# A two-stage graph network on one core: one-pass batch statistics, a normalisation folded into weights, merged matrix products, and a last stage spread over three engines

## The chip, the core and the metric

The kernel runs on 1 core of a Trainium2 chip. The metric is the device time of one launch in microseconds (us). Below, PE is TensorE, DVE is VectorE, ACT is ScalarE, POOL is GpSimd and SP is SyncE, which here only starts transfers. All numbers are fp32.

## What is computed

12,500 nodes with 64 values each, 400,000 edges sorted by `dst` with 32 values each. Three passes over the edges, with weights between them:

```python
# layer 0
msg  = relu(concat([x[dst], x[src], edge_attr, u_per_node[dst]]) @ W1 + b1)
agg  = segment_sum(msg, dst)
x    = layernorm(x + relu(concat([x, agg, u_per_node]) @ W2 + b2))
# layers 1 and 2: h starts as x
def _egnn_conv(h, src, dst, ea, W, b, bias):          # ea = edge_attr @ We + be
    h = h @ W + b
    return relu(segment_sum(h[src] + ea, dst) + h) + bias
def _batchnorm(x, gamma, beta):                       # over all 12,500 nodes
    mu, var = mean(x, axis=0), var(x, axis=0)
    return (x - mu) * rsqrt(var + EPS) * gamma + beta
h = _batchnorm(_egnn_conv(x, ...1), g1, beta1)
h = _batchnorm(_egnn_conv(h, ...2), g2, beta2)
return layernorm(x + h)
```

`u_per_node` is one row for all nodes, since `batch` is all zeros.

## The kernel before, in words

The core runs through a start, and then three times (l = 0, 1, 2) through an edge loop and a node stage. Every engine has its own program; semaphores tie them together, and each engine works its own list in order.

**Start.** DVE and PE find where each block of 128 nodes begins among the edges. POOL gathers rows of `dst` for it (98 gathers, L530) and, when the ranks are known, scatters node rows into the table `ranked` (98, L538). Beside this PE forms, for 14 groups of 7 blocks, three products per block (L602 to L604): node rows by W1's first half, a product of `glob_b` (the row u with a 1 behind it) by `w_glob`, which adds u's share and the bias, and node rows by W1's second half. SP loads `xt`, a group at a time.

**Edge loop** (625 steps of 5 tiles of 128 edges). In each step POOL starts 5 indirect DMAs (L556) that gather source rows of 128 edges each from `source_table`. The ring `message` holds 10 steps. DVE makes the one-hot matrix `hit` (L937), PE multiplies (L666), DVE adds the result into `by_rank` (L952). In layer 0 PE also forms the edge products (L639, L642), with a one-hot `spread` from DVE (L925).

**Node stage** (14 groups of 7 blocks of 128 nodes). PE transposes `by_rank` (L678), ACT copies it out (L762), SP stores it to `sums`. POOL fetches a node's sum by its rank: it copies the ranks of a group from `rank_i` into `node_idx` (L569) and gathers 7 times (L574). DVE builds `cat` from what was fetched (L964, or L968 to L974), PE transposes it (L689), ACT copies the transpose to `cat_t` (L770), PE multiplies by the node weights (L701 to L703 in layer 0, where L703 is again the product of `glob_b`; L705 in layers 1 and 2), DVE applies the relu (L983, L988). In layer 0 a layernorm follows (`after_norm`, L810 to L820, with a square root on ACT, L776) and SP stores the group as the next `source_table`. The groups are pipelined: `fetched` and `cat` have two halves.

**Batch statistics** (layers 1 and 2). PE adds up `conv` over the partitions, a group at a time, with a matrix of ones (L711), one group behind. At the end DVE has the mean (L1015), subtracts it from all 14 groups (L1022), ACT squares each (L789), PE sums the squares (L724), DVE reduces (L1027), ACT takes the root (L794), DVE the reciprocal and the gain (L1029, L1030). In layer 1 DVE then scales and shifts all of `conv` in 7 pairs of groups (L1034, L1035), SP stores each pair as the next `source_table` (L494) and behind the last one loads the first indices (L409). In layer 2, DVE works through 7 pairs: gain, beta, add xn, and a layernorm (L1043 to L1045, then L813 to L820), with a root on ACT (L799); SP writes the pairs out (L500, L502).

The order is written out by hand. The lines that decide the starts named later:

```python
# SP, before the edge loop of layers 1 and 2
if l:
    sp.wait_ge(tile_summed[l - 1], STEPS)
    for n in range(0, CYCLE, TURN):
        load_index(Step(0, n))
    wait_for_table(sp, l)
```

## Time and profile before

| | us |
|---|---|
| time before, median of 3 runs (12688.62 to 12696.25) | 12688.88 |
| the profiled execution, its own time | 12692.79 |
| its span, on which all sums below are made | 12691.0 |
| busy POOL / PE / DVE / ACT | 9386.9 / 6733.1 / 4907.3 / 395.8 |
| first POOL gather of the three edge loops | 300.1, 4448.7, 8545.1 |
| last POOL gather of the three edge loops | 4239.6, 8348.2, 12444.5 |

So some 300 us are the start, three loops of 3900 to 3940 us follow, and after each a node stage: about 209 us, 197 us and 246 us (to the end at 12691.0). Times are microseconds from the span's start unless marked ns. In a timeline row the first number is the start, the second the duration; the bracket is the engine's idle time before it and what ended it. A row "x2" or "x7" covers so many instructions. An fp32 product shows as two matmul records.

### The profile page before, as it was taken

Reading aid. Unit: us, or ns where it says so; the run is one execution under the profiler, and the core shown is the slowest. Engines: PE = TensorE matmul, PEld = TensorE weight load, DVE = VectorE, ACT = ScalarE, POOL = GpSimd, SP = SyncE. Lnnn points to the kernel's source line nnn. Section 1 sums busy time; section 2 is a strip of 40 time slices with the busy share of each in tenths; the row PEclk is TensorE's granted clock in tenths of the full one; section 3 lists DMA queues with packets and bytes.
Section 4 is the critical chain, followed back from the end, with each engine's and each line's share of the span. In section 5 each row is a group of like instructions: output and inputs, shape, how many; then the busy total and the mean of one; then the engine's idle time right before and its main releaser. Section 6 shows DMA issues by size and latency. Waiting matters only on the chain.

```text
span 12691.0 us, 121543 instructions
## 1 busy us (share of the span) xinstructions
PE 6733.1 (53%) x29865; PEld 5780.0 (46%) x29865; DVE 4907.3 (39%) x12980; ACT 395.8 (3%) x790; POOL 9386.9 (74%) x9927
## 2 busy tenths in 40 slices
PE   4888877888878833333333333343333333333334
PEld 4777766677767733333333333333333333333333
DVE  2444444444444333333333333333333333333334
ACT  0000000000000100000000000000000000000000
POOL 6777777777777577777777777767777777777774
PEclk9666667666666555555555555555555555555555
DMA  2444434343444222222222222221111111111111
GB/s 78 100 94 93 95 93 96 92 95 92 98 94 94 65 41 40 41 40 40 40 40 40 41 40 40 40 54 27 27 27 27 27 27 27 27 27 27 27 27 37
DMA packets 1598914, 688.43 MB, mean 54 GB/s; under 512 B 1359841, under 2 KB 1422977, under 8 KB 1598734
## 3 DMA queue, kind: packets, MB, share of 16 engines
q0 software_dynamic: 315680, 328.70, 13.3%
q1 hardware_dynamic: 1283181, 359.10, 12.8%
q8 instruction: 24, 0.39, 0.0%
q14 instruction: 29, 0.24, 0.0%
HBM read 658.74 MB, written 28.14 MB: 54 GB/s over the span
## 4 chain that ended last, share of the span: by engine, by line
POOL 32%; PE 28%; DMA 19%; issue 15%; DVEq 3%; DVE 2%; POOLq 0%; ACT 0%; SPq 0%; ACTq 0%
POOL message L556 30%; PE sum_ps L666 20%; DMA message<-source_table,index 18%; PE pre_ps L642 3%; DVEq L920 3%; PE pre_ps L639 2%; POOL fetched L574 1%; DVE by_rank L952 1%; POOL ranked L538 1%; DVE summed_in L931 0%; PE out_ps L701 0%; PE out_ps L703 0%; PE out_ps L702 0%; PE sum_ps L689 0%; DMA xt<-in_x_t 0%
## 5 line engine op out<-in xcount | busy, mean ns | idle before, releaser
L556 POOL DMA_INDIRECT message<-source_table,index x9375 | 8887.3, 948 | 2947.0 <-issue 2546.7
L666 PE MATMUL sum_ps<-hit,message 128*64 128x128 f32 (+1 forms) x18750 | 4254.6, 408 | 4821.3 <-DMA message<-source_table,index 4746.6
L666 PEld LDWEIGHTS sum_ps<-hit,message 128*64 128x64 f32 (+1 forms) x18750 | 3577.4, 231 | 5348.2 <-DMA message<-source_table,index 4962.0
L952 DVE TENSOR_TENSOR by_rank<-by_rank,sum_ps 64x128 f32 (+1 forms) x9375 | 2628.5, 280 | 4567.1 <-PE sum_ps L666 4277.6
L937 DVE TENSOR_TENSOR hit<-out_ps,edge_place 128x640 f32<-128x640 f32 x1875 | 1526.8, 814 | 1207.2 <-PE sum_ps L666 690.6
L639 PE MATMUL pre_ps<-w_edge,scratch 96*128 96x192 f32 x2500 | 946.9, 473 | 874.6 <-DVE summed_in L931 742.0
L642 PEld LDWEIGHTS pre_ps<-scratch 128*128 128x128 f32 x6250 | 1230.9, 271 | 111.5 <-issue 79.0
L642 PE MATMUL pre_ps<-scratch 128*128 128x64 f32 x6250 | 1278.4, 356 | 0.0
L639 PEld LDWEIGHTS pre_ps<-w_edge,scratch 96*128 96x128 f32 x2500 | 525.5, 262 | 1119.3 <-DVE summed_in L931 790.6
L931 DVE TENSOR_TENSOR summed_in<-pre_ps,message 128x320 f32<-128x320 f32 x625 | 303.1, 485 | 771.7 <-issue 594.1
L925 DVE TENSOR_SCALAR scratch<-edge_cat,lane 128x640 f32<-128x640 bf16 x625 | 344.9, 552 | 603.2 <-issue 593.1
L750 ACT ACTIVATE message<-summed_in 128x320 f32<-128x320 f32 x625 | 293.6, 470 | 3788.2 <-DVE summed_in L931 3756.9
L574 POOL DMA_INDIRECT fetched<-sums,node_idx x294 | 285.4, 971 | 139.9 <-issue 76.8
L762 ACT COPY message<-sum_ps 128x448 f32<-128x448 f32 (+1 forms) x21 | 12.5, 594 | 7869.8 <-PE sum_ps L678 7845.4
L530 POOL DMA_INDIRECT xn<-in_dst_rows,tile_of x98 | 108.8, 1111 | 50.9 <-issue 29.3
L689 PE MATMUL sum_ps<-ident,cat 128*98 128x128 f32 x294 | 71.8, 421 | 100.5 <-DVE cat L974 94.0
L538 POOL DMA_INDIRECT ranked<-by_rank,place x98 | 93.9, 958 | 41.0 <-issue 29.6
L689 PEld LDWEIGHTS sum_ps<-ident,cat 128*98 128x98 f32 x294 | 53.2, 197 | 107.8 <-DVE cat L974 97.8
L705 PEld LDWEIGHTS out_ps<-w_cat,cat_t 98*128 98x128 f32 x392 | 72.0, 275 | 26.3 <-ACT cat_t L770 26.2
L914 DVE MEMSET by_rank<- 128x12672 f32 x3 | 31.9, 10618 | 120.5 <-issue 120.5
L701 PE MATMUL out_ps<-w_2a,cat_t 64*128 64x64 f32 x196 | 62.5, 421 | 16.3 <-ACT cat_t L770 13.8
L705 PE MATMUL out_ps<-w_cat,cat_t 98*128 98x64 f32 x392 | 70.1, 355 | 2.0 <-ACT cat_t L770 2.0
(153 smaller groups left out, 1270.3 us busy)
## 6 DMA issues: line engine op xcount, KB each, us to landing
message<-source_table,index POOLq DMA_INDIRECT x9375
edge_cat<-place_rows SPq DMA_DIRECT2D x125, 800.0 KB
scratch<-ranked SPq DMA_DIRECT2D x3125, 32.0 KB
scratch<-in_edge_t_steps SPq DMA_DIRECT2D x125, 480.0 KB, 4.6
message<-in_edge_steps SPq DMA_DIRECT2D x625, 80.0 KB, 2.5
xt<-in_x_t SPq DMA_DIRECT2D x28, 224.0 KB, 3.6
index<-in_src_steps SPq DMA_DIRECT2D x375, 12.5 KB
fetched<-sums,node_idx POOLq DMA_INDIRECT x294, 2.5
```

The costliest lines, as they stand in the source:

```text
L538: nc.gpsimd.indirect_dma_start(ranked[:, :], bass.IndirectOffsetOnAxis(ap=place[:, b:b + 1], axis=0), terms[:, b, :], None).then_inc(ranke ...
L556: nc.gpsimd.indirect_dma_start(to, None, source_table[l][:, :], bass.IndirectOffsetOnAxis(ap=index[:, at.j, s:s + 1], axis=0))\
L574: nc.gpsimd.indirect_dma_start(fetched[:, h, q, 0:width[l]], None, sums[l][0:(g + 1) * GB * P, :], bass.IndirectOffsetOnAxis(ap=node_idx[: ...
L639: mm(pre_ps[:, m.half, q * F:(q + n) * F], eat[0:n * C, m.j // TURN, m.part, q // STACK, :], w_edge[0:n * C, 0:n * F], start=True, stop=False)
L642: one = mm(pre_ps[:, m.half, s * F:(s + 1) * F], spread[:, m.half, s, :], window[:, m.part, s, :], start=False, stop=(s == q + n - 1))
L666: one = mm(tile_sum(at.half, s)[0:w, :], of, hit[:, at.half, s, :], start=True, stop=True)
L750: nc.scalar.activation(active[:, at.half, :, :], summed_in[:, at.half, :, :], ACT.Relu).then_inc(message_made, 1)
L920: dve.reg_load(add_regs, tile_ranks[:, bass.ds(at.number * S, TURN * S)])
L925: V.tensor_scalar(spread[:, o.half, :, :].rearrange("p s e -> p (s e)"), place_row[:, o.j // TURN, o.part, :], lane[:, 0:1], None, ALU.is_ ...
L931: V.tensor_tensor(summed_in[:, m.half, :, :], pre_ps[:, m.half, 0:S * F].rearrange("p (s f) -> p s f", f=F), rows[:, m.slot, :, :], ALU.add)\
L937: V.tensor_tensor(hit[:, m.half, :, :], over(along_ps, [P, S, P], 1), over(edge_place[:, bass.ds(m.number * S, S)], [P, S, P], 2), ALU.is_ ...
L952: V.tensor_tensor(at_rank[s], at_rank[s], tile_sum(at.half, s)[0:w, :], ALU.add)\
```

## The change

- **Ranks as node indices**: `node_idx` and its copy (L569) are gone; the gathers take `rank_i` as it is.
- **Merged products**: the product of `glob_b` is made once, and its row is placed as a 65th row in `w_ab` and `w_2x`; `xt` gets a 65th row of ones. In the start one 128-column product per block replaces three of 64 columns; in layer 0's node stage two products per block replace three.
- **One-pass statistics**: the mean of group 0 (over its 896 rows) is taken as a guess and subtracted from `conv` at once, by the bias of the relu from group 1 on. DVE keeps a running total of the groups (`total`) and of their squares (`square_total`), which ACT squares one group behind. PE sums over partitions once at the end. The variance is the mean of squares less the square of the mean.
- **Layer 1's normalisation folded**: `conv` is stored unscaled, group by group, as `source_table[2]`; gain and shift go into `w_cat[1]` (PE transposes gain and shift, DVE scales the rows and adds the shift's share).
- **Index loads** of layers 1 and 2 stand behind the edge loop before, ahead of the stores of `sums`.
- **Last stage on three engines**: POOL adds the shift to xn, DVE scales, adds, centres and reduces, ACT squares, takes the roots, and does the last scaling (14 instructions of 64 columns a pair); DVE does it for the last pair.

```diff
+            V.memset(xt[F:F + 1, :, :], 1.0)
+            V.memset(w_ab[F:F + 1, F:2 * F], 0.0)
+            dve.wait_ge(globals_ps, 1)
+            V.tensor_copy(w_ab[F:F + 1, 0:F], out_ps[F:F + 1, 0:F])
+            V.tensor_copy(w_2x[F:F + 1, :], out_ps[F:F + 1, F:2 * F]).then_inc(globals_kept, 1)
...
-                    mm(to[:, q * P:q * P + F], xb, w_ab[:, 0:F], start=True, stop=False)
-                    mm(to[:, q * P:q * P + F], glob_b[:, :], w_glob[0][:, :], start=False, stop=True)
-                    last_mm = mm(to[:, q * P + F:(q + 1) * P], xb, w_ab[:, F:2 * F], start=True, stop=True)
+                    last_mm = mm(to[:, q * P:(q + 1) * P], xt[:, h, q * P:(q + 1) * P], w_ab[:, :], start=True, stop=True)
...
-                                mm(to, xt[:, h, q * P:(q + 1) * P], w_2x[:, :], start=False, stop=False)
-                                one = mm(to, glob_b[:, :], w_glob[1][:, :], start=False, stop=True)
+                                one = mm(to, xt[:, h, q * P:(q + 1) * P], w_2x[:, :], start=False, stop=True)
...
-                    nc.gpsimd.tensor_copy(node_idx[:, h, :], rank_i[:, g * GB:(g + 1) * GB]).then_inc(idx_copied[l], 1)
-                    pool.wait_ge(idx_copied[l], g + 1)
...
-                            bass.IndirectOffsetOnAxis(ap=node_idx[:, h, q:q + 1], axis=0))\
+                            bass.IndirectOffsetOnAxis(ap=rank_i[:, g * GB + q:g * GB + q + 1], axis=0))\
...
+                if l == 2:
+                    pool.wait_ge(square_used[1], NG + 1)
                 pipeline(pool, steps)
...
+            pool.wait_ge(shift_known, 2)
+            for i in range(NG // 2):
+                pair = slice(i * 2 * GB, (i + 1) * 2 * GB)
+                nc.gpsimd.tensor_tensor(xn[:, pair, :], xn[:, pair, :], over(mean[:, :], [P, 2 * GB, F], 1), ALU.add)\
+                    .then_inc(shift_added, 1)
...
-                    for g in range(NG // 2):
-                        sp.wait_ge(conv_ready, g + 1)
+                    for g in range(NG):
+                        sp.wait_ge(node_kept[1], g + 1)
...
+                    pe.wait_ge(totalled[l], NG)
+                    mm(stat_ps[:, 0:GW], ones[:, :], total, start=True, stop=False)
+                    mm(stat_ps[:, (GB - 1) * F:GW], unreal[:, :], conv[:, NB - 1, :], start=False, stop=True)
+                    pe.wait_ge(square_used[l], NG + 1)
+                    mm(square_ps, ones[:, :], square_total, start=True, stop=False)
+                    mm(square_ps[:, (GB - 1) * F:GW], unreal[:, :], square[1][:, GB - 1, :], start=False, stop=True)\
                         .then_inc(stat_done, 1)
...
+            def last_scale(i):
+                act.wait_ge(last_recip_made, i + 1)
+                for b in range(i * 2 * GB, (i + 1) * 2 * GB):
+                    one = nc.scalar.activation(conv[:, b, :], conv[:, b, :], ACT.Copy, scale=t[4][:, b:b + 1])
+                one.then_inc(final_made, 1)
+
+            for i in range(NG // 2):
+                pair = slice(i * 2 * GB, (i + 1) * 2 * GB)
+                act.wait_ge(last_centred, i + 1)
+                wait(act, last_var_made, i - 1)
+                nc.scalar.activation(last_square[i % 2], conv[:, pair, :], ACT.Square).then_inc(last_squared, 1)
+                if i == NG // 2 - 1:
+                    last_root(i)
+                if i:
+                    last_scale(i - 1)
+                if i < NG // 2 - 1:
+                    last_root(i)
...
+                            link(V.tensor_tensor(bias, bias, mean[:, :], ALU.add))
+                        else:
+                            add_squares(g - 1, 1 - h, l)
...
+                            V.tensor_tensor(total, total, flat, ALU.add).then_inc(totalled[l], 1)
```

DVE in the pipelined groups of layer 2's node stage, one group, before. `cat` is the input of group g; L988 is the relu of group g - 1.

```order
L970 TENSOR_TENSOR cat<-fetched,some 128x7x64
L972 ISA
L972 COPY cat<-edge_cat 128x7x34
L271 REGISTER_ALU
L974 ISA
L974 TENSOR_TENSOR cat<-cat,scratch 128x7x64
L980 ISA
L988 ISA
L988 SCALAR_TENSOR_TENSOR scratch<-out_ps,rows_b 128x448
```

The same place now; L1061 adds the squares of the group before, and `total` lies in the buffer of `message`.

```order
L1016 TENSOR_TENSOR cat<-fetched,some 128x7x64
L1018 COPY cat<-edge_cat 128x7x34
L290 REGISTER_ALU
L1020 TENSOR_TENSOR cat<-cat,scratch 128x7x64
L1036 SCALAR_TENSOR_TENSOR scratch<-out_ps,rows_b 128x448
L1061 TENSOR_TENSOR hit<-hit,summed_in 128x448
L1054 TENSOR_TENSOR message<-message,scratch 128x448
```

Two additions of 448 columns, both with two inputs in SBUF, follow the relu in every group.

DVE in the last stage, one pair of groups, before (the address arithmetic between them left in as it stands):

```order
L1043 TENSOR_TENSOR message<-scratch,gain 128x896
L1044 TENSOR_TENSOR message<-message,rows_b 128x896
L1045 TENSOR_TENSOR message<-message,xn 128x896
L813 TENSOR_REDUCE m<-message 128x14
L814 TENSOR_SCALAR m<-m 128x14
L815 TENSOR_TENSOR message<-message,m 128x896
L816 TENSOR_TENSOR message<-message 128x896
L817 TENSOR_REDUCE m<-message 128x14
L819 RECIPROCAL m<-m 128x14
L820 TENSOR_TENSOR scratch<-message,m 128x896
```

And now, from the second pair on:

```order
L1127 TENSOR_TENSOR message<-scratch,gain 128x896
L1129 TENSOR_TENSOR message<-message,xn 128x896
L1112 TENSOR_REDUCE t2<-message 128x14
L1132 TENSOR_REDUCE t0<-message 128x14
L1133 TENSOR_SCALAR t1<-t0 128x14
L1134 TENSOR_TENSOR scratch<-message,t1 128x896
L1118 RECIPROCAL t4<-t3 128x14
```

Eight DVE instructions of 896 columns a pair have become five; L1112 and L1118 belong to the pair before. ACT in the same stage, now:

```order
L837 ACTIVATE message<-scratch 128x896
L830 ACTIVATE scratch<-scratch,t4 128x64 x14
L824 ACTIVATE t3<-t2,eps 128x14
L837 ACTIVATE message<-scratch 128x896
L824 ACTIVATE t3<-t2,eps 128x14
L830 ACTIVATE scratch<-scratch,t4 128x64 x14
```

The square (L837) and the 14 scalings (L830) of the pair before have moved here from DVE; in the last pair the root (L824) goes ahead of the scalings.

## Rows read from the trace of the kernel before

**Rows 1.** The POOL gathers of the three edge loops: duration min/median/max in ns, first and last start.
```profile
L556 POOL DMA_INDIRECT message<-source_table,index x3123: 940/944/1454, 300.1 to 4239.6; - x196
...
L556 POOL DMA_INDIRECT message<-source_table,index x3125: 940/944/962, 4448.7 to 8348.2; - x196
...
L556 POOL DMA_INDIRECT message<-source_table,index x3125: 940/944/961, 8545.1 to 12444.5; - x196
```
**Rows 2.** Timeline of the start: the end of PE's products and POOL's last gather.
```profile
160.87 0.63 PE L604 MATMUL pre_ps<-w_ab,xt 64*128 64x64 f32 x2
...
162.70 0.94 POOL L530 DMA_INDIRECT xn<-in_dst_rows,tile_of  x1 [0.30 <-ACT fetched L741]
```
**Rows 3.** Layer 0's node stage: a group of instructions, then two pieces of the chain.
```profile
L703 PE MATMUL out_ps<-w_glob,glob_b 33*128 33x64 f32 x196 | 61.9, 418 | 0.0
...
4284.94 1.68 PE sum_ps L689 x7
...
4296.81 1.68 PE sum_ps L689 x7
```
**Rows 4.** The chain in the node stages of layers 1 and 2: first gathers of groups.
```profile
8360.56 0.97 POOL fetched L574
...
8487.11 0.97 POOL fetched L574
...
12474.56 0.97 POOL fetched L574
...
12578.36 0.97 POOL fetched L574
```
**Rows 5.** Timeline of layer 1's node stage: a gather beside DVE's instructions.
```profile
8488.18 0.63 DVE L970 TENSOR_TENSOR cat<-fetched,some 128x448 f32<-128x448 f32 x1
8488.38 1.24 POOL L574 DMA_INDIRECT fetched<-sums,node_idx  x1 [0.30 <-issue]
8488.72 0.39 DVE L972 COPY cat<-edge_cat 128x238 f32 x1
8489.03 0.62 DVE L974 TENSOR_TENSOR cat<-cat,xn 128x448 f32<-128x448 f32 x1
```
**Rows 6.** Layer 1's end: two timeline rows, a transfer's time to landing, then the next loop's first gather.
```profile
8502.75 1.81 PE L705 MATMUL out_ps<-w_cat,cat_t 98*128 98x64 f32 x14
8504.59 0.62 DVE L988 SCALAR_TENSOR_TENSOR scratch<-out_ps,rows_b 128x448 f32<-128x448 f32 x1 [4.38 <-PE out_ps L705]
...
source_table<-xn SPq DMA_DIRECT2D x14, 224.0 KB, 2.4
...
8545.12 0.94 POOL message L556
```
**Rows 7.** Timeline of layer 2's end.
```profile
12593.11 3.08 PE L705 MATMUL out_ps<-w_cat,cat_t 98*128 98x64 f32 x14
...
12596.91 1.86 PE L711 MATMUL stat_ps<-scratch,ones 128*128 128x448 f32 x2 [0.72 <-DVE scratch L988]
...
12599.13 0.62 DVE L1015 TENSOR_REDUCE mean<-stat_ps 128x64 f32<-128x448 f32 x1 [2.27 <-PE stat_ps L717]
...
12618.14 1.09 DVE L1043 TENSOR_TENSOR message<-scratch,gain 128x896 f32<-128x896 f32 x1
```
**Rows 8.** Timeline of the last stage: first pair's root, reciprocal, scaling; last pair's scaling.
```profile
12626.22 0.31 ACT L799 ACTIVATE m<-m,eps 128x14 f32<-128x14 f32 x1 [8.95 <-DVE m L817]
12626.55 0.24 DVE L819 RECIPROCAL m<-m 128x14 f32<-128x14 f32 x1 [0.37 <-ACT m L799]
12626.83 1.09 DVE L820 TENSOR_TENSOR scratch<-message,m 128x896 f32<-128x896 f32 x1
...
12685.55 1.09 DVE L820 TENSOR_TENSOR scratch<-message,m 128x896 f32 x1
```
**Rows 9.** Groups of instructions: ACT's and POOL's prices by width.
```profile
L770 ACT COPY cat_t<-sum_ps 98x896 f32<-98x896 f32 x14 | 12.7, 905 | 129.9 <-PE sum_ps L689 129.9
...
L520 POOL TENSOR_SCALAR_AFFINE_SELECT tri<-tri 128x128 f32<-128x128 f32 x1 | 0.3, 282 | 0.0
```

228 lines of the change are left out of this document (145 added, 83 removed).

## The prediction, made before the changed kernel ran

> **What bounds the kernel now.** I read the gathers of the edge loops first. They fill three stretches, 300.1 to 4239.6, 4448.7 to 8348.2 and 8545.1 to 12444.5, with 3125 gathers each and a median of 944 ns [rows 1]. In the second and third, 3899.5 / 3124 = 1.248 us pass from one gather to the next: 0.94 and a fixed gap of 0.31. POOL paces them and nothing else does. The first is 40 us longer; its longest gather took 1454 ns against 962, so something delays single gathers there. No edit touches an instruction of these loops, so 11,740 of 12,691 us stay. What can move is the start and the three node stages, some 950 us together, and there I followed the chain that ended last, stage by stage.
>
> **The start: nothing.** The merged product takes 14 x 7 x 3 products down to 14 x 7. But PE ended at 161.5 while POOL, which had its own 98 gathers to issue, began the last one at 162.70 [rows 2], and 98 scatters follow on POOL. The row names an ACT copy as the releaser of that gather, after the usual gap of 0.30, so it is a coincidence of times. A PE that ends 60 us earlier meets a POOL that is as late as before. I take 0. The two new products of `glob_b` and the four small DVE instructions lie ahead of PE's first load of `xt`, where both engines idle. If POOL did wait there, 1 or 2 us either way.
>
> **Layer 0's node stage: 42 us.** Here the chain alternates between PE and one copy on ACT. From one group's transposes to the next it is 4296.81 - 4284.94 = 11.87 [rows 3], of which 1.68 are transposes, 0.91 ACT's copy [rows 9], some 0.3 hand-overs, and the remaining 9.0 are 21 products, 0.43 each. The product of `glob_b` is a third of them (its 196 records stand in rows 3 for 14 groups): 3.0 a group, 42 in 14. What is next late is POOL. Its 7 gathers take 7 x 1.25 = 8.75 and delays; PE will need 11.9 - 3.0 = 8.9, and POOL is two groups ahead when PE begins. So the whole 42 should come. If POOL needed 9.4 a group (as now, below) and its lead were used up, 36 would; that is the low end. The index load, now ahead, saves some tenths behind it.
>
> **Fetching by rank without the copy: 4 us, from -8 to 18.** In layers 1 and 2, POOL's gathers are the chain from 8360.56 and from 12474.56 on. A group takes (8487.11 - 8360.56) / 13 = 9.73 in layer 1, (12578.36 - 12474.56) / 11 = 9.44 in layer 2 [rows 4]. Seven gathers are 8.74, so the copy with its two waits costs 0.70 a group. 13 groups would give 9.1 in each layer: 18. But the change puts two DVE additions of 448 columns into every group, and those delay gathers. In [rows 5] L970 runs from 8488.18 to 8488.81; the gather that began at 8488.38 took 1.24, 0.30 more than its 0.94, and ended 0.81 after L970 did. So a gather needs something, 0.13 after its start, that DVE holds while it reads two SBUF operands. The additions are 0.62 long like L970 and L974 [rows 5], and a moment that falls evenly over 1.25 meets such an instruction with a mean delay of 0.62 x 0.62 / 2.5 = 0.15. Four of them give 0.6 a group, where today layer 1 shows 0.30 and layer 2 none. The expected balance is 0.70 - 0.3 = 0.4 in layer 1 and 0.70 - 0.6 = 0.1 in layer 2, 6 together; since the phase is nearly the same in each group, it isn't an average but a lottery. Laying DVE's list beside the gathers from 1.3 after a group's first start, I find three hits in layer 1 (1.2) and two in layer 2 (0.7), which gives -6. I take 4.
>
> The Trainium skill says the same of the mechanism (SBUF — State Buffer, Who interferes with whom): a DVE instruction with two SBUF inputs contends with a GpSimd instruction that reads SBUF, one waiting for the whole of the other. The trace agrees, with its 0.30. By that rule this edit is worth less than its copy and could be a loss; by a reading of the copy alone it would be 18.
>
> **Layer 1's end: 35 us.** The relu of the last group ends at 8505.21, and the next loop's first gather is at 8545.12 [rows 6]: 39.9 for mean, centring, squares, scaling and a store. Now only the store of the last group stands between: 2.4 to landing [rows 6] and some 1.0 to the gather, 3.4. POOL also waits for the last addition of squares, which is ready 2.0 to 2.4 after the relu (ACT's square 0.6, three additions of 0.65), as late as the store at most. That is 36.5. Against it: the products of the last group took 1.81 at layer 1's end and 3.08 at layer 2's [rows 6, 7], and without the wide column sums (L711) PE will have less to do before them; I take 1.3 off, a bound of 0 to 1.3. What becomes late instead: DVE and PE still have statistics, folding and the clearing of `by_rank` to do, some 12 + 11 = 23 after the relu by the rows of layer 2's end. POOL doesn't feel it, since the ring takes 10 steps of 6.24, 62 us, and PE and DVE need under 4 of the 6.24 a step to catch up.
>
> **Layer 2's end: 11.5 us.** Before, from PE's first sum (12596.91) to the first scaling (12618.14) it is 21.2 [rows 7]. After: the last addition of squares 2.0 behind the relu; PE's two pairs of products, the first started at 1.4, each 2.2 as from 12596.91 to 12599.13 [rows 7], so to 5.6; two reductions of 0.65, four small instructions of 0.25, a root of 0.4, a reciprocal of 0.6, three small ones: 9.8. The gain is 11.5, 9 if each hand-over costs 0.3 more.
>
> **The last stage: 16.5 us, from 9 to 21.** Seven pairs took (12685.55 - 12626.83) / 6 = 9.79 each [rows 8], with 8 instructions of 1.09, two small ones, a root, and nothing beside them. Now DVE has 5 x 1.13 + 0.21 + 0.27 = 6.1 a pair. ACT has a square of 0.95 (by the 905 ns for 896 columns [rows 9]), a root of 0.31 and 14 scalings of 64 columns. The line through 0.31 at 14 columns [rows 8] and 0.905 at 896 gives 0.34 each; with overlap, as L970 and L972 do (0.63 long, the next starts 0.54 later [rows 5]), 0.25. Then ACT needs 4.8 to 6.3 and DVE leads or is level; I take 6.1. The first pair 5.1, six more 36.6. POOL's seven additions read two SBUF operands. No row has their price: 0.28 for 128 columns [rows 9], of which a fixed part may be 0.1, makes 0.3 to 1.4 for 896. They hold up DVE for nothing, if they fit under its reductions, up to 7 x 1.4 = 10; I take 3. Behind the last centring come a square, a reduction, a root, then ACT's 14 scalings of the pair before and only then that pair's store: 5.4 to 7.4, against 3 before, and two large stores queue at the end where one did, for which 12691.0 - 12686.6 = 4.4 passed [rows 8]; with both I take 6.1. So 5.1 + 36.6 + 3 = 44.7 to the last centring, 5.4 + 6.1 = 11.5 behind it, 56.2 for 72.9 (12618.14 to 12691.0): 16.7, taken as 16.5.
>
> The Trainium skill gives 4497 ns for 2048 columns of such an addition (GPSIMD Engine Reference, Elementwise — side-by-side cycle accounting), an estimate of 2.0 us here; no run shows it yet. By it the last stage would be 1 to 4 us longer and the time near 12582.
>
> **The sum.** 42 + 4 + 35.2 + 11.5 + 16.5 = 109.2. The profiled span of 12691.0 goes to 12581.8, its own time of 12692.79 to 12583.6. The median is 3.9 below that execution, so 12688.88 - 109.2 = 12579.7; I say 12579.5.
>
> **Rivals.** *Fetching gets its full 18* (the two additions fall between the gathers' sensitive moments): 12566. For it: layer 2 shows no delay today though L970 and L974 run there; against it, four instructions are harder to miss. *The last stage gains half*, because POOL and DVE hold each other up or ACT's scalings are the pace at 0.34 and more: 12588 to 12592. For it is that nothing in the trace runs there beside DVE now. *Layer 0 falls to POOL's pace*: 9.4 a group, 12585. *The early start of the last loop is given back*: if DVE and PE lag by more than the ring's 62 us, the loop stalls until they have caught up; at a lag of 25 it costs nothing, at 90 some 28: 12608. *Slower*: all gathers of the loops lose pace. The first loop shows the mechanism, 40 us by delays of single gathers, 13 ns on each of 3125. To end over 25 us above the time before, all 9375 must lose (109 + 25) / 9375 = 14.3 ns, more than the first loop shows, in all three; as no instruction of DVE in the loops changes, only their phase against POOL could do it. *It doesn't do what it says*: the last loop starts only when the fold is done, because its first gathers wait for more than the store; the fold ends some 12 behind the relu, not 3.4, so 12588, within the range.
>
> **Chances.** Forecast with its small terms 0.66, full fetch saving 0.08, half a last stage 0.14, layer 0 at POOL's pace 0.04, late start or gain given back 0.05, within 0.2% (25 us, about what a measurement can tell here from no change) 0.02, slower 0.01. The bounds of the terms, -12 for fetching, 7.5 for the last stage, 6 for layer 0, 5 for the first loop's 40 us of delays, don't all fall one way; root of squares about 15. Two thirds of the cases lie within 12565 to 12594; taking in the rivals next to them, the range is 12557 to 12601.
>
> **What would show it.** Three gaps between loops: 209 should become 167, 197 become 158, and from 12444.5 to the end 246 become 218. In the fetches, a group of 9.3 to 9.5 with gathers over 1.2 us long beside the new additions; at 8.75 the rival holds. In layer 0, 8.9 a group on PE. First gather 3.4 behind layer 1's last relu. In the last stage 6.1 between DVE's centrings; longer and with gaps behind POOL, or with DVE waiting for ACT's root, the second rival. If the gathers' cadence in the loops differs from 1.248, what I take as fixed is wrong, and with it everything.

## The result, and the profile after

The changed kernel takes 12608.87 us (median of 4 runs, 12606.95 to 12610.91) where the kernel before, run beside it, took 12688.75: ratio 0.9937, 95% interval 0.9925 to 0.9948. It is faster by 80 us, not by 109, and 12608.87 lies 8 us above the forecast's range. The profiled execution has a span of 12605.2 us; before it was 12691.0, so 85.8 less. (The profiled execution of before lay 4.0 above its median, this one 1.9 below. So 23 of the 29 us that are missing from the forecast stand in the table below, and the other 6 are in the choice of executions.)

The loops first, as in [rows 1]: the gathers of the three edge loops, with duration min/median/max in ns, first and last start.

```profile
L579 POOL DMA_INDIRECT message<-source_table,index x3125: 940/945/1452, 295.8 to 4235.2; - x196
...
L579 POOL DMA_INDIRECT message<-source_table,index x3125: 940/944/962, 4433.9 to 8334.2; - x196
...
L579 POOL DMA_INDIRECT message<-source_table,index x3125: 940/944/962, 8486.2 to 12386.6; - x196
```

The cadence is what it was: 3900.3 and 3900.4 us for 3124 steps, against 3899.5. What moved lies between. ([rows 1] lacks two of the 3125 gathers of the first loop; by the timeline it runs from 298.9 to 4240.8.)

| stretch, us | before | after | moved | forecast |
|---|---|---|---|---|
| start to the first gather | 298.9 | 295.8 | -3.1 | 0 |
| three edge loops | 11740.9 | 11740.1 | -0.7 | 0 |
| layer 0's node stage | 207.9 | 198.7 | -9.2 | -42 |
| layer 1's node stage: first to last fetching gather | 134.4 | 124.8 | -9.5 | } -4 |
| layer 2's, the same | 130.2 | 126.5 | -3.7 | } |
| layer 1's stage, the rest | 62.5 | 27.2 | -35.3 | -35.2 |
| layer 2's stage to the first scaling, the rest | 43.5 | 31.5 | -11.9 | -11.5 |
| last stage, first scaling to the end | 72.9 | 60.5 | -12.3 | -16.5 |

**Layer 0** holds the miss. The chain that ended last, in one group (start, us, what), where [rows 3] stood before:

```profile
4325.95 0.92 ACT cat_t L795
4326.91 0.69 PE out_ps L728 x2
4327.60 0.62 PE out_ps L729 x2
4328.22 0.62 PE out_ps L728 x2
...
4335.61 1.51 PE sum_ps L718 x7
4337.22 0.92 ACT cat_t L795
```

A group takes 4337.22 - 4325.95 = 11.27 us, 0.6 less than before. There are 14 products where there were 21, but behind the first each takes 0.62 instead of 0.43. From the first start to the last end the products of a group take 8.7 us, where they took 9.2. The timeline shows the rhythm: weights (PEld) are loaded for 0.50, and the next load starts only 0.61 after this one, alternately for 64 and for 65 rows.

```profile
4331.23 0.50 PEld L729 LDWEIGHTS out_ps<-w_2x,xt 65*128 65x128 f32 x2
4331.23 0.69 PE L729 MATMUL out_ps<-w_2x,xt 65*128 65x64 f32 x2
4331.84 0.50 PEld L728 LDWEIGHTS out_ps<-w_2a,cat_t 64*128 64x128 f32 x2
4331.85 0.69 PE L728 MATMUL out_ps<-w_2a,cat_t 64*128 64x64 f32 x2
```

**Fetching** has groups of 8.74 to 9.36 us, shorter than those of before [rows 4]. Still, 11 gathers in layer 1 and 19 in layer 2 take over 1.0 us instead of 0.94, 3.8 and 5.4 us in all. SBUF and PSUM are the core's two on-chip memories; PE's results land in PSUM. Laid beside DVE's instructions, each of these 30 gathers falls on one with two operands in SBUF that had begun before it, and it is longer by what was left of that instruction 0.13 after the gather's start, to within 0.014. Who begins first counts. In 29 of the 30 cases DVE began 0.05 or more ahead, in one 0.02; 17 other gathers met such an instruction that began between 0.03 before and 0.13 after their own start, and none of them took over 0.95. Two places of the timeline, on the older line L1016 (as in [rows 5]) and on the new addition L1054:

```profile
12428.50 1.15 POOL L597 DMA_INDIRECT fetched<-sums,rank_i  x1 [0.30 <-issue]
12428.75 0.62 DVE L1054 TENSOR_TENSOR message<-message,scratch 128x448 f32<-128x448 f32 x1
...
12444.07 0.62 DVE L1016 TENSOR_TENSOR cat<-fetched,some 128x448 f32<-128x448 f32 x1 [6.01 <-DMA fetched<-sums,rank_i]
12444.17 1.34 POOL L597 DMA_INDIRECT fetched<-sums,rank_i  x1 [0.30 <-issue]
```

In both layers together, 14 gathers meet one of the two new additions (5.1 us) and 16 an older instruction (4.0 us; before there were 12, 4.1 us, all in layer 1).

**Layer 1's end.** The relu of the last group, the last store, and the next loop's first gather, which waited for that store (compare [rows 6]):

```profile
8482.17 0.62 DVE L1036 SCALAR_TENSOR_TENSOR scratch<-out_ps,rows_b 128x448 f32<-128x448 f32 x1 [4.47 <-PE out_ps L731]
...
8482.82 0.36 SPq L514 DMA_DIRECT2D source_table<-scratch  x1
...
8486.24 0.94 POOL L579 DMA_INDIRECT message<-source_table,index  x1 [14.00 <-DMA source_table<-scratch]
```

8486.24 - 8482.79 = 3.4 us behind the relu, as forecast.

**The last stage.** The first two pairs, engines DVE and POOL, and then POOL's additions by duration (min/median/max in ns):

```profile
12544.67 1.09 DVE L1127 TENSOR_TENSOR message<-scratch,gain 128x896 f32<-128x896 f32 x1
12544.72 18.54 POOL L605 TENSOR_TENSOR xn<-xn,mean 128x896 f32<-128x896 f32 x7 [19.33 <-DVE mean L1097]
12547.79 2.87 DVE L1129 TENSOR_TENSOR message<-message,xn 128x896 f32<-128x896 f32 x1 [2.03 <-POOL xn L605]
12550.69 1.09 DVE L1132 TENSOR_REDUCE t<-message 128x14 f32<-128x896 f32 x1
12551.82 0.81 DVE L1133 TENSOR_SCALAR t<-t 128x14 f32<-128x14 f32 x1
12552.66 2.91 DVE L1134 TENSOR_TENSOR scratch<-message,t 128x896 f32<-128x896 f32 x1
12555.60 2.85 DVE L1127 TENSOR_TENSOR message<-scratch,gain 128x896 f32<-128x896 f32 x1
12558.49 2.84 DVE L1129 TENSOR_TENSOR message<-message,xn 128x896 f32<-128x896 f32 x1
...
L605 POOL TENSOR_TENSOR xn<-xn,mean x7: 2065/2917/2965, 12544.7 to 12560.3; 128x896 f32<-128x896 f32 x7
```

POOL's seven additions took 18.54 us, 2.65 on the mean, and that mean hides two kinds: two took 2.06 and 2.07, five 2.91 to 2.97. While they ran, four of DVE's two-operand instructions took 2.84 to 2.91 instead of 1.09. The fifth, the first L1127, began 0.05 before POOL's first addition and kept its 1.09. The reductions (one operand) stayed at 1.09. The first pair's centring ends 10.9 after the first scaling begins, the second's 9.2 later, the other five come every 5.7.

### The profile page after: what moved, and what is told of

Its sections match the earlier page's. It is cut to its first block, busy times and chain, and to the rows that moved or that the text cites. A ratio compares the mean times of both kernels' runs of the same rounds, so it can differ in the third digit from the quotient of the medians.

```text
span 12605.2 us, 120022 instructions
## 1 busy us (share of the span) xinstructions
PE 6639.1 (53%) x29185; PEld 5681.8 (45%) x29185; DVE 4898.2 (39%) x13002; ACT 419.5 (3%) x881; POOL 9398.5 (75%) x9892
## 4 chain that ended last, share of the span: by engine, by line
POOL 32%; PE 28%; DMA 19%; issue 15%; DVEq 3%; DVE 2%; POOLq 0%; ACT 0%; ACTq 0%; SPq 0%
POOL message L579 29%; PE sum_ps L695 21%; DMA message<-source_table,index 18%; PE pre_ps L671 3%; DVEq L966 3%; PE pre_ps L668 3%; POOL fetched L597 1%; DVE by_rank L998 1%; POOL xn L553 1%; POOL ranked L561 1%; DVE summed_in L977 1%; PE out_ps L728 0%; PE out_ps L729 0%; DMA sums<-hit 0%; PE sum_ps L718 0%
## 5 line engine op out<-in xcount | busy, mean ns | idle before, releaser
L971 DVE TENSOR_SCALAR scratch<-edge_cat,lane 128x640 f32<-128x640 bf16 x625 | 344.9, 552 | 604.8 <-issue 592.5
L597 POOL DMA_INDIRECT fetched<-sums,rank_i x294 | 288.9, 983 | 145.1 <-issue 82.6
L728 PE MATMUL out_ps<-w_2a,cat_t 64*128 64x64 f32 x196 | 67.2, 445 | 16.8 <-ACT cat_t L795 13.8
```

The source lines that it names most:

```text
L597: nc.gpsimd.indirect_dma_start(fetched[:, h, q, 0:width[l]], None, sums[l][0:(g + 1) * GB * P, :], bass.IndirectOffsetOnAxis(ap=rank_i[:, ...
L971: V.tensor_scalar(spread[:, o.half, :, :].rearrange("p s e -> p (s e)"), place_row[:, o.j // TURN, o.part, :], lane[:, 0:1], None, ALU.is_ ...
```

## Experiments

Theory: three causes cost time that this kernel could do without, one for each place above, and they don't depend on each other. (The first is more than all that is missing; fetching is ahead of its forecast even so.) (1) PE pays 0.19 us whenever a product of at most 64 rows and one of more than 64 follow each other. (2) A gather is held by a DVE instruction with two SBUF operands, and by nothing else of DVE. (The second half doesn't hold, as shown under fetching.) (3) The same conflict, at full length, between DVE and POOL in the last stage. The rivals stand with each run. On some chips transfers land later: there the kernel before took 16,179 us (16,185 and 16,339 in two other sets), and groups of gathers wait for them (in the run below in which DVE adds the shift, POOL stood 990 us in front of the loops' gathers for index loads, in 62 waits; in the changed kernel that wait isn't among its large ones). From runs there I take only durations and waits on the engines. The two kernels that change the last stage alone, and the three cures together without the shorter end, ran only there; the others ran on a chip at the usual pace too.

### Layer 0: rows of the two products

```diff
-        w_2a = sb("w_2a", [F, F])
+        w_2a = sb("w_2a", [F + 1, F])
...
+            V.memset(w_2a[F:F + 1, :], 0.0)
...
-                                mm(to, cat_t[0:F, h, q * P:(q + 1) * P], w_2a[:, :], start=True, stop=False)
+                                mm(to, cat_t[0:F + 1, h, q * P:(q + 1) * P], w_2a[:, :], start=True, stop=False)
```

> The changed kernel with one edit: in layer 0's node stage the product of cat_t also has 65 rows (w_2a gets a 65th row of zeros, cat_t is read to row 64, whose column of cat is zero in this layer), so the two products of a node block have the same number of rows. Theory A (the alternation between products of 64 and of 65 rows costs 0.19 us at each switch): a product takes 0.43 again instead of 0.62, a group on PE 14 x 0.43 + 2.9 = 8.9 instead of 11.2, the gap between the first two loops falls from 198.7 to 167 or, if POOL's gathers are then the pace at 9.3 a group, to 172; time 12577 to 12582. Theory B (a product of 65 rows is slow in itself, 0.81 against 0.43): all fourteen take 0.81, a group 14.2, time 12650. Theory C (the two products of a block wait for each other because they accumulate in the same place): unchanged, 11.2 a group, 12608.

Measured: 12573.85 us (12571.39 to 12575.68), 35 less than the changed kernel. The chain:

```profile
4314.48 0.92 ACT cat_t L795
...
4315.44 0.69 PE out_ps L728 x2
4316.12 0.43 PE out_ps L729 x2
4316.55 0.43 PE out_ps L728 x2
```

More rows, and each product faster: 0.43 at 65 and 65. A group takes 8.8 us, POOL's own pace (8.74 for seven gathers) is nearly reached, and the stage falls to 164.0. A group's products take 6.2 us instead of 8.7: 13 changes of 0.19. Theories B and C are out. The stage is now 43.9 below that of before, where 42 was forecast. The second kernel keeps 64 and 65 rows and only sorts (with it, `start` and `stop` are given once a group and not once a product):

```diff
+                            for q in range(GB):
+                                mm(out_ps[:, q * F:(q + 1) * F], cat_t[0:F, h, q * P:(q + 1) * P], w_2a[:, :],
+                                   start=(q == 0), stop=False)
+                            for q in range(GB):
+                                one = mm(out_ps[:, q * F:(q + 1) * F], xt[:, h, q * P:(q + 1) * P], w_2x[:, :],
+                                         start=False, stop=(q == GB - 1))
```

> The changed kernel with one edit: in layer 0's node stage the seven products of 64 rows of a group go first, then the seven of 65 rows, which leaves 2 switches a group of 14. Theory A (0.19 us at each switch): 2 x 0.19 + 14 x 0.43 + 2.9 = 9.3 a group, the gap between the first two loops 172, time 12582. Theory B (65 rows slow in itself): unchanged, 11.2 a group and 12608. Theory C (the second product of a block waits for the first, since both accumulate in one place): seven other products now lie between, so 8.9 a group, 12577; A and C are told apart by the one-row-count kernel, which leaves the order as it is.

Measured: 12574.70 us (12573.05 to 12581.08), the stage 166.8.

```profile
4314.88 0.91 ACT cat_t L799
...
4315.84 3.25 PE out_ps L727 x14
4319.09 3.18 PE out_ps L730 x14
4322.26 1.51 PE sum_ps L718 x7
...
4323.86 0.92 ACT cat_t L799
```

8.98 us a group, beside the 9.3 of theory A and the 8.9 of theory C, which the first run had ruled out. The products take 6.4 us. Inside them there is 1 change instead of 13, and it shows as 0.19 on top of the 6.2; the other, from the transposes to the first product, falls into the wait for ACT's copy. It is the change that costs, not the 65th row. In time the two kernels, 12573.85 and 12574.70, are the same. The third run looks from the other side: the kernel before, with 65, 64 and 33 rows in turn instead of 64, 64 and 33.

> The kernel before with a 65th row in the product of cat_t in layer 0, once more at the gathers' own pace. On a chip with late transfers its groups took 14.4 where 11.97 was the period of before. Theory (0.19 us for each of 14 changes of row count): 12689 + 10 to 13 groups of 2.5 + the first groups, of which POOL's lead hides up to 8: 12715 to 12726. Rival (other work takes it up): 12689.

Measured: 12721.81 us (12712.97 to 12726.61) beside 12688.57, ratio 1.0027 (1.0017 to 1.0037). Its first two products of a block are the slow ones:

```profile
4337.35 0.69 PE out_ps L701 x2
4338.03 0.62 PE out_ps L702 x2
4338.65 0.43 PE out_ps L703 x2
4339.07 0.62 PE out_ps L701 x2
```

L701 (65 rows) comes after 33, L702 (64) after 65: each pays 0.19. L703 (33 after 64) pays nothing. A group takes 14.4 us instead of 11.97, its products 11.7 instead of 9.2: again 13 changes of 0.19. Row counts of 33 and 64 are one kind, 64 and 65 two; counts between 33 and 64 were not tried. The same kernel on a chip with late transfers (16213.47 us beside 16185.46) showed the same 14.4.

### Fetching: operands in PSUM, and the copy put back

```diff
-                            V.tensor_tensor(total, total, flat, ALU.add).then_inc(totalled[l], 1)
+                            V.tensor_tensor(total if isinstance(g, int) and g == NG - 1 else running, running, flat, ALU.add).then_inc(totalled[l], 1)
...
-                    V.tensor_tensor(square_total, square_total, of, ALU.add).then_inc(square_used[l], 1)
+                    V.tensor_tensor(square_total if isinstance(g, int) and g == NG - 1 else running_square, running_square,
+                                    of, ALU.add).then_inc(square_used[l], 1)
```

`running` and `running_square` are free banks of PSUM.

> The changed kernel with one edit: the two running sums of layers 1 and 2 (the additions of a group to total and to square_total) are kept in PSUM instead of SBUF, so each addition reads one operand in SBUF and one in PSUM; only the last addition of a layer writes to SBUF. DVE does as many instructions, of the same size, at about the same moments. Theory A (a gather is held up by a DVE instruction with two SBUF operands, and by nothing else of DVE): the gathers over 1.0 us beside the additions go; of the 5.4 us of excess in layer 2's fetching and the 3.8 in layer 1's some 5 and 2 go, fetching falls from 126.5 to 121.5 and from 124.8 to 123, time 12602. Theory B (any busy DVE delays a gather, or the excess comes from something else): no change, 12608. If reading PSUM makes an addition longer (say 0.8 for 0.63), nothing of the time hangs on it, as DVE has idle time in each group.

Measured: 12605.8 us (12603.03 to 12615.63). Fetching takes 122.8 and 125.0 for 124.8 and 126.5. The time isn't apart from the changed kernel's by more than the spread of the runs; the trace says more. None of the long gathers lies on an addition any more (14 did); the 20 that are left, 1.7 and 4.0 us, lie on the instructions that are L1016 and L1020 in the changed kernel and their like, where it had 16. The cause is right. Layer 1 is where it was expected (123), layer 2 isn't (121.5): the older instructions now meet more gathers than they did. So all of DVE's operands had to go: mask, masked rows and sums in PSUM.

```diff
+        running, running_square = stat_ps[:, 0:GW], sum_ps[:, 0, 0:GW]
+        masked = sum_ps[:, 1, 0:GW].rearrange("p (q f) -> p q f", f=F)
+        some_ps = pre_ps[:, 1, 0:NB]
...
-                    mask = some[:, blocks]
+                    mask = some_ps[:, blocks]
...
-                        V.tensor_tensor(cat[:, h, :, 0:F], cat[:, h, :, 0:F], (xn if l == 1 else conv)[:, blocks, :],
+                        V.tensor_tensor(cat[:, h, :, 0:F], masked, (xn if l == 1 else conv)[:, blocks, :],
...
+                dve.wait_ge(rank_kept[l], NG)
+                link(V.tensor_copy(some_ps, some[:, :]))
```

> The changed kernel with one edit, wider than the one of the running sums: in the node stages of layers 1 and 2 the mask `some`, the masked rows and both running sums lie in PSUM, so in a group no DVE instruction reads two operands in SBUF (one copy of `some` to PSUM a layer is added, where DVE waits anyway). Theory A (only a DVE instruction with two SBUF operands delays a gather; in the changed kernel's fetching I count 14 gathers on the new additions, 5.1 us, and 16 on the older instructions, 4.0 us): all of it goes but one on the centring of the first group, periods are 8.74, fetching takes 121.3 to 121.8 in both layers where it took 124.8 and 126.5, time 12600 to 12601. Theory B (the older instructions delay gathers in another way): periods stay at 8.9 to 9.2 as in the kernel with the running sums alone, 12605.

That run fell on a chip with late transfers (16058.30 us), where none of the 196 gathers of layers 1 and 2 was long; the repeat gives time too:

> The changed kernel with mask, masked rows and running sums of the fetching in PSUM, once more at the gathers' own pace. Theory: periods of 8.74, fetching 121.3 in both layers for 124.8 and 126.5, time 12608.9 - 8.7 = 12600. Rival (delays by late landing, not by DVE, make up part of the 124.8 and 126.5): 12605.

Measured: 12602.88 us (12601.30 to 12605.35), 6 less than the changed kernel. The fetching gathers of layers 1 and 2:

```profile
L600 POOL DMA_INDIRECT fetched<-sums,rank_i x98: 940/944/954, 8342.4 to 8471.1; - x98
...
L600 POOL DMA_INDIRECT fetched<-sums,rank_i x98: 940/944/961, 12396.9 to 12520.8; - x98
```

The longest of 196 takes 961 ns; in the changed kernel it is 1409. That isn't for want of meetings: 20 of them began while a DVE instruction with one operand in PSUM and one in SBUF was running, with over 0.2 us of it left. Groups are 8.74 apart but for one a layer, 16.4 and 11.6:

```profile
8364.56 0.26 DVE L1087 COPY pre_ps<-some 128x98 f32<-128x98 f32 x1 [27.92 <-ACT hit L790]
...
8367.52 0.94 POOL L600 DMA_INDIRECT fetched<-sums,rank_i  x1 [7.93 <-DVE cat L1025]
```

That wait is my own: the mask's place in PSUM is free only when ACT has copied the last rank group, so DVE starts late, and POOL, which may be two groups ahead and no more, waits 7.93. Without it the layers would be at 121.1, so the delays by DVE were worth 3.7 + 5.4 = 9.1, all that the long gathers had shown.

The "nothing else of DVE" of the theory is refuted by a place that nobody edited. In layer 0's edge loop L971 takes one tensor from SBUF, with a column of scalars, and writes to SBUF:

```profile
1236.37 0.54 DVE L971 TENSOR_SCALAR scratch<-edge_cat,lane 128x640 f32<-128x640 bf16 x1
1236.38 1.34 POOL L579 DMA_INDIRECT message<-source_table,index  x1 [0.30 <-issue]
```

In the changed kernel 94 gathers of that loop began while L971 was running with over 0.2 us left, and 84 of them took over 1.0. Of all DVE instructions in that loop it is the one that most of the long gathers meet (104 of 174), and so a part of the 39 us by which the first loop is longer than the others. No run here takes it away.

The copy of the ranks put back into the changed kernel:

```diff
+                    nc.gpsimd.tensor_copy(node_idx[:, h, :], rank_i[:, g * GB:(g + 1) * GB]).then_inc(pool_step, 1)
+                    pool.wait_ge(pool_step, 7 + l * NG + g + 1)
```

> The changed kernel with the copy of the ranks put back, once more at the gathers' own pace. On a chip with late transfers its undisturbed groups took 9.44 to 9.94, with 9 to 15 gathers of over 1.0 a layer, so the phase is no better than without the copy. Theory A (0.70 a group on top of about the same delays): fetching takes 134 and 136, time 12627. Theory B (the copy moves the gathers off DVE's instructions): 12613 to 12621.

Measured: 12620.52 us (12617.17 to 12623.38), 11.7 more than the changed kernel; fetching takes 134.7 and 133.4, 16.8 more.

```profile
8438.82 0.20 POOL L595 COPY node_idx<-rank_i 128x7 int32<-128x7 int32 x1
8439.80 0.97 POOL L600 DMA_INDIRECT fetched<-sums,node_idx  x1 [0.78 <-POOL node_idx L595]
```

The time lies where theory B had it (12613 to 12621); the trace says A with one correction. 26 copies of 0.70 are 18.2, and 16.8 came, since the delays are 1.4 us less in all: both layers together are 7.7 above the 130.2 of a layer with copies and no long gather (layer 2 of the kernel before), where the changed kernel has 9.1. On two chips with late transfers (16058.17 and 16043.67 us) it showed the same copy and 24 to 26 long gathers. The time rose less than the fetching; the rest of this execution was 6.6 us shorter (3.6 of it in the loops), which no edit explains. The runs of one changed kernel lie 4 to 14 us apart. One of the long gathers lies on a copy of 448 columns from SBUF to SBUF (0.39 long, the gather 1.06), a second instruction with one operand that holds gathers; in the changed kernel the copy of 238 columns (L1018) held none of the 7 that met it.

### The last stage

DVE adds the shift itself, POOL does nothing:

```diff
-                dve.wait_ge(shift_added, i + 1)
+                link(V.tensor_tensor(last_sum, last_sum, over(mean[:, :], wide, 1), ALU.add))
```

> The changed kernel with one edit: in the last stage POOL adds nothing; DVE adds the shift of the second normalisation itself, one more instruction of 896 columns a pair. Theory A (DVE's instructions of the first two pairs took 2.85 instead of 1.09 because POOL's additions ran beside them): the first centring ends 6.1 after the first scaling begins (before 13.8 for the first centring's end, and 20 for the second), each further one 6.8 later, the last after 47 where it was 48.6; time 12607. Theory B (they are long from something else, ACT's squares or stores beside them): the two long pairs stay and seven instructions of 1.09 come on top, 56 to the last centring, time 12616.

This and the next run fell on a chip with late transfers (16092.95 and 16083.67 us), but no transfer is waited for between the first scaling and the last centring. By line, in that stretch:

```profile
L1124 DVE TENSOR_TENSOR message<-message,xn 128x896 f32<-128x896 f32 x7 | 7.6, 1092 | 0.2
...
L1123 DVE TENSOR_TENSOR message<-message,mean 128x896 f32<-128x896 f32 x7 | 7.6, 1091 | 0.2
...
L1128 DVE TENSOR_SCALAR t<-t 128x14 f32<-128x14 f32 x7 | 1.2, 175 | 0.2
```

All at 1.09, the stretch 46.8 us for 48.6. Theory A holds: POOL's help cost more than the 7 x 1.09 it saved. Then POOL kept, and DVE's sum and gain moved to PSUM:

```diff
-        last_sum = ring[:, 0:2 * GW].rearrange("p (q f) -> p q f", f=F)
+        last_sum = sum_ps.rearrange("p h n -> p (h n)")[:, 0:2 * GW].rearrange("p (q f) -> p q f", f=F)
...
+                    of_gain = gain[:, :] if l == 1 else out_ps[:, 0:F]
```

> The changed kernel with one edit: in the last stage the intermediate sum and the gain lie in PSUM, so each of DVE's instructions there reads at most one operand in SBUF (scaling: conv in SBUF and gain in PSUM; addition: sum in PSUM and xn in SBUF; centring: sum in PSUM and means in SBUF). POOL still makes its seven additions of two SBUF operands beside them. Theory A (DVE and POOL hold each other up only when DVE reads two SBUF operands): no DVE instruction is over 1.2 us; the first addition waits for POOL's first (2.0 to 2.6), so the first centring ends some 6 us after the first scaling begins and each further one 5.7 later, the last after 40 to 41 where it was 48.6; POOL's additions get shorter than 2.65 too; time 12600. Theory B (POOL's additions stretch any DVE instruction): the two long pairs stay, 12608.

```profile
16024.93 14.28 POOL L605 TENSOR_TENSOR xn<-xn,mean 128x896 f32<-128x896 f32 x7 [25.91 <-DVE mean L1098]
16027.10 1.10 DVE L1130 TENSOR_TENSOR sum_ps<-sum_ps,xn 128x896 f32<-128x896 f32 x1 [1.14 <-POOL xn L605]
...
16029.36 1.72 DVE L1134 TENSOR_SCALAR t<-t 128x14 f32<-128x14 f32 x1
```

POOL alone needs 2.04 an addition, DVE's wide instructions are back at 1.09, and the stretch is 42.1. A surprise is L1134: 14 columns, one tensor operand, 0.17 long without POOL, and it took 1.72 here and 0.56 in the second pair. The next kernel tests that by keeping the row sums in PSUM. It also shortens the end: ACT scales four blocks of the last pair but one before the last root, and the last pair's stores go ahead of the other's. It has the cures of layer 0 and of the fetching in it too.

```diff
-                link(V.tensor_scalar(t[1][:, pair], t[0][:, pair], 1.0 / F, None, ALU.mult))
+                link(V.tensor_scalar(t[1][:, pair], out_ps[:, P:P + 2 * GB], 1.0 / F, None, ALU.mult))
...
+                    last_scale(i - 1, range(4))
+                    last_root(i)
+                    last_scale(i - 1, range(4, 2 * GB))
```

> The kernel with the three cures and two edits more, both in the last stage. First, the row sums that are scaled to means lie in PSUM too: with the sum in PSUM two of these small DVE instructions, 0.17 long, still took 1.72 and 0.56 beside POOL. Theory A (an instruction that has all its operands in SBUF and runs in a fast mode is held up as well): both go back to 0.17, 1.9 us. Theory B (POOL's addition holds them by its semaphore, not by SBUF): they stay. Second, the end: ACT scales four blocks of the last pair but one before the last root, where it idled 1.15, and the last pair's stores are issued ahead of the last but one's; the last ACT scaling ends 1.0 earlier, and the 6.2 from there to the end becomes some 4.5: 2 to 3 us. Together 12558.7 - 4.5 = 12554; if the final stores are bound by their own bytes, 12556.

```profile
16025.42 0.17 DVE L1148 TENSOR_SCALAR t<-out_ps 128x14 f32<-128x14 f32 x1
```

With its operand in PSUM it is back at 0.17, so theory A holds; the stretch is 40.2, and 9.8 us instead of 11.9 follow the last centring. The chip was one with late transfers again (16068.68 us; the three cures without these two edits 16071.49, with 42.1 and 11.9).

### Do the parts add up?

> The kernel with all cures and the shorter end once more. On the chips of the last runs every kernel, that of before among them, took some 16,100, because their transfers landed later; the parts could be read there but not their worth in time at the gathers' own pace. If the parts add up as read: 12608.9 - 35 (layer 0) - 8.7 (fetching) - 8.4 (last stage to the last centring, 40.2 for 48.6) - 2.1 (end, 9.8 for 11.9) = 12554.7. Rival: early ends of fetching are lost at the layers' ends: 12563. On another slow chip, again only the parts can be read.

Measured: 12558.42 us (12557.08 to 12560.19) beside 12688.57, ratio 0.9897 (0.9881 to 0.9914); 50.5 less than the changed kernel where 54.2 was expected. The last stage is the one just shown (40.2 and 9.8). The wait found above, which this kernel has in all three layers (16.3 us for one group in layer 1, 10.8 in layer 2, 11.0 in layer 0), takes more than what is missing: by the traces fetching is at 128.6 and 123.1 and has gained 0 instead of 9. Start and loops are 3.9 shorter than in the changed kernel's execution, which no edit explains. The last kernel lets the first two groups of a layer read the mask from SBUF and copies it to PSUM behind them:

```diff
-                    mask = some_ps[:, blocks]
+                    mask = (some if isinstance(i, int) and i == 0 else some_ps)[:, blocks]
```

> The kernel with all cures, without its own wait for the rank copies, once more, since the run before fell on a chip with late transfers. 12558.4 less 7.5 (layer 1), 2.0 (layer 2) and 2.2 (layer 0): 12547; the third group's period 8.7 to 9.2 in all three layers. Rival: the wait moves to the mask's new place, periods over 10 at the fourth group, 12550 to 12558.

Measured: 12553.95 us (12551.89 to 12556.48) beside 12686.13, ratio 0.9897 (0.9880 to 0.9913).

```profile
L601 POOL DMA_INDIRECT fetched<-sums,rank_i x98: 940/944/995, 8314.3 to 8437.5; - x98
...
L601 POOL DMA_INDIRECT fetched<-sums,rank_i x98: 940/944/962, 12363.4 to 12484.5; - x98
```

Fetching is 121.1 in layer 2, every group 8.74. In layer 1 it is 123.2, as 2.1 of the wait moved to the mask's new place, one group later. So the 12547 was missed, and the rival (12550 to 12558) is what came. Layer 0 takes 164.8. The traces give 128.6 - 123.2 = 5.4 and 123.1 - 121.1 = 2.0 less; the medians differ by 4.5. This is the fastest of the kernels on chips at the usual pace: 132 us below the kernel before, 55 below the changed one. (A first run of it, on a chip with late transfers, took 16231.28.)

## Why the prediction was wrong

- **Layer 0, 42 forecast, 9 came: the step that failed.** "the remaining 9.0 are 21 products, 0.43 each" was read rightly, and 7 of the products went. The step from there to "PE will need 11.9 - 3.0 = 8.9" took it that the price of a product stays when its neighbour changes. Before, a block's products had 64, 64 and 33 rows; merging put a 65th row (the ones) into one of two, and 13 changes of 0.19 a group came in, 2.5 for the 3.0 saved. (The transposes behind them take 1.51 for the 1.68 of [rows 3]: they have 128 rows, and before they followed one of 33.) That alone is worth 35 us by the run with 65 and 65 rows, more than the whole miss of 29, and with it the stage gains 43.9, the 42 of the forecast. So the reading, the overlap with POOL and the count of products held; the price was wrong. The rival for this stage, POOL's pace of 9.4, was the wrong one: the groups went at PE's 11.27. The Trainium skill has a rule against this change that I passed over (TensorEngine Tiling (Array Packing), Tiling Modes, Key Properties): a change of the tiling mode drains the engine, and the configurations listed there have 128, 64 or 32 rows, so that 33 and 64 rows would fit one and 65 needs another. It doesn't say that a plain product falls under it and has no price. The traces agree in kind, with 0.19 us each; that a drain is what takes the 0.19 no run shows.
- **The start, 0 forecast, 3.1 came.** PE ended its first products at 95 instead of 161.5 us, and POOL's last gather there began at 160.24 instead of 162.70 [rows 2]. "As late as before" was nearly right.
- **Fetching, 4 forecast (-8 to 18), 13.2 came.** The copy's 0.70 was right (18.2; 16.8 in the run that puts it back). The mechanism against it was right too, but the 14 taken off for new delays measured 5.0 (5.1 on the new additions). The step that mis-sized it is the mean of 0.15 for each instruction. It counts the whole 0.62, though the same paragraph reads that a gather waits only for what is left 0.13 after its start. With 0.62 - 0.13 = 0.49 the mean is 0.49 x 0.49 / 2.5 = 0.10, four are 0.38 a group, and the balance is 13 x (0.70 - 0.38 + 0.30) + 13 x (0.70 - 0.38) = 12.2. Measured are 9.1 / 104 = 0.09 for each instruction (0.07 in layer 1, 0.10 in layer 2), so a little of that agreement is luck. The -6 from laying the lists side by side, which drew the term down to 4, pointed the wrong way: the same two or three moments are met in most groups, and of the 44 new additions made while the gathers ran, 30 held none.
- **Layer 1's end, 35.2 forecast, 35.3 came**, with all its steps: 3.4 from relu to gather; the last group's products 3.25 instead of 1.81 [rows 6], 1.4 more, for which I had taken 1.3. In the last 3 us (8502 to 8505 before, 8479 to 8482 after) the profile shows the granted clock: 0.83 before (both levels in one stretch, 1.2 and 2.4 GHz) and 0.50 (1.2 GHz) after. Ahead of that, PE made the wide column sums before and none after. That they are the reason isn't shown: at layer 2's end of the kernel before, with the same sums, the products took their 3.08 at 0.50.
- **Layer 2's end, 11.5 forecast, 11.9 came.** From the first scaling back to the last relu it is 9.1.
- **The last stage, 16.5 forecast (9 to 21), 12.3 came.** The steps after POOL were right: 5.7 a pair (forecast 6.1), 11.9 behind the last centring (11.5). The step that failed is POOL's hold-up of DVE, taken as 3 of at most 10; it was 9.3: (10.9 - 5.1) + (9.2 - 5.7), and the additions took 2.04 alone and 2.65 on the mean beside DVE, for which I had 0.3 to 1.4. They didn't fit under the reductions: each two-operand instruction of DVE that met one waited for its end. The result lies halfway between the forecast and the rival "gains half", whose mechanism it shows. The Trainium skill's figure, from which I had the estimate of 2.0 (GPSIMD Engine Reference, Elementwise — side-by-side cycle accounting), fits the 2.04 closely; this term was off by 4, and 1 to 4 more would have mended it, but not the sum, which layer 0 had put 33 off.
- **Loops, 0 and 0.** The cadence held, and the early start of the last loop was not given back.

## What to carry to other kernels

Before products are merged or a row is added to one, look at the row counts of the products that alternate with it: two kinds in turn can cost as much as the product saved, and a row of zeros or another order gives it back. Where POOL sets the pace, gathers or additions, keep one operand of DVE's two-operand instructions in PSUM beside it; PSUM banks that lie idle do for running sums, masks and row statistics. A single operand in SBUF isn't safe by itself: look in the trace whether copies and TENSOR_SCALARs from SBUF to SBUF meet long gathers too. When delays are priced as a mean over phases, subtract from the length the part of the meeting that costs nothing. A free place has a time from which it is free: look at who must wait for it before a cure is priced.

## What was not expected of the hardware

- A product of 65 rows beside one of 64: 0.62 us instead of 0.43 for either, at 64 moving columns and a granted clock of 0.50 (1.2 GHz). 33 beside 64 costs nothing.
- DVE's 1.09 us instructions of 896 columns and two SBUF operands took 2.84 to 2.91 beside POOL's additions, and five of POOL's took 2.91 to 2.97 instead of 2.04. DVE waited 1.8 of POOL's 2.04, POOL 0.9 of DVE's 1.09: whoever comes second waits nearly for the whole of the other.
- A DVE TENSOR_SCALAR of 14 columns, operand and result in SBUF, took up to 1.72 us for 0.17 beside POOL, and 0.17 once it read PSUM. The Trainium skill (SBUF — State Buffer, Who interferes with whom) counts `tensor_scalar` among the instructions that can enter a mode in which DVE takes the pair of ports shared with GpSimd. The runs agree, with 1.72 and 0.17; whether these 14 columns ran in such a mode they don't show. The same section infers that a `tensor_tensor` leaves the generation of a DMA's descriptors alone; here 30 of 196 gathers took up to 1.41 beside one, and the measurement decides.
- A gather waits for a DVE instruction with two SBUF operands that began before it, for what is left of it 0.13 us after the gather's start (30 gathers, within 0.014), and not for one that begins with it or later (17 gathers). With one operand in PSUM: 0 of 196 over 1.0 us. One operand doesn't make it safe: beside L971 84 of 94 gathers were long.
- Chips differ: the same kernel before took 12,686 to 12,690 us in four sets of runs and 16,179 to 16,339 in three, on other chips, with gathers of the same 0.94 us each. In the run on such a chip named above POOL stood 990 us before the loops' gathers for index loads, 1235 us for what the view calls remote, and 3867 instead of 2545 us for nothing that the profile shows. So late transfers are a part; what makes the chips so is open.
